# Rows spread to alternating channels, and zero products between the first maxima, in a two-layer gated attention and expert kernel

## The chip, the cores and the metric

The kernel runs on one core of one Trainium2 chip. The metric is the device time of one execution in microseconds, the median of several runs. The engines are named as in the profile: PE is the matrix engine (PEld its weight loads), DVE the vector engine, ACT the scalar engine, POOL the general engine, and SP the engine whose queue issues every DMA transfer of this kernel. Layers are counted 0 and 1, batches 0 to 7.

## The reference

The computation is two layers on x (8 batches of 100 tokens, 128 channels), each a cross-attention to a context of 1444 keys and then a mixture of experts:

```python
x = x + tanh(g_xattn[0]) * attention0(layernorm(x), ctx, mask)
x = x + tanh(g_ffn[0])   * experts0(layernorm(x))     # 64 experts of 64 channels, 8 per token, one shared
x = x + tanh(g_xattn[1]) * attention1(layernorm(x), ctx, energy gate)
x = x + tanh(g_ffn[1])   * experts1(layernorm(x))     # 8 experts of 352 channels, 2 per token
```

Attention has 16 heads of 8 channels with a softmax over the keys. An expert computes `down(silu(gate(x)) * up(x))`; a token's result is the sum over its experts, weighted with its routing weights. Both layers' experts are computed for all tokens, with weight 0 where a token is not routed to an expert.

## The kernel before

Each engine runs its own program, written out by hand; the order of an engine's instructions is the order in the code, and semaphores tie the engines together. There is no scheduler. The whole program is attention(0), experts(0), attention(1), experts(1).

**Attention.** For every batch, PE first finds the row maxima of the scores, head by head. A quad of maxima (`max_quad`, L1349) is four products of 100 x 482 into the four banks of `pm`; DVE takes them in two halves (`quad_max`, L487) into `mx_part`. A batch has 12 quads. From batch 1 on, the quads lie between the score products of the batch ahead (in `slots`). Those of batch 0 come ahead of everything, in the loop at the end of PE's `attention`: all 12 in layer 0, with three projections of keys (`k_chunk`) between them, and the last 8 in layer 1, since the first 4 are done inside experts(0) (`early_max`, L1556). After them `max_rows` turns the maxima, and the twelve slots of each batch follow: scores (L1405) to one of the two `ps` banks, exponent on ACT, weighted values on PE (L1426).

**Experts.** Channels are cut into units of 128: in layer 0 a unit is two experts of 64 channels, with the shared expert as the 33rd; in layer 1 there are 22 units. Tokens are cut into halves a and b (400 tokens), so layer 0 has 66 passes and layer 1 has 44, and pass n is called unit n here. Each unit goes round the engines:

- SP brings its weights (`wts`, a ring of 7, L1760) and its rows of routing weights (`wb`, a ring of 5, L1771 in layer 0, L1775 in layer 1). `wb` holds, for each of the 128 channels, the 400 routing weights of the expert that this channel belongs to. It comes from the array `routing` in DRAM, where an expert has one row of 400. SP issues the rows of unit n+5 when unit n has been weighted, and the weights of unit n+7 when the last product of unit n is done.
- ACT and DVE split the weights in a high and a low part (L1128, L648), PE multiplies (six products, L1611), ACT applies silu (L1136), DVE multiplies gate and up (L659).
- POOL multiplies the result with `wb` (`weigh`, L951, L961), and two units later PE adds the down product to the sum (`down`, L1640).

The layer-0 transfer is written so that the source is two rows, each repeated 64 times, and the outermost dimension has 2 entries:

```python
sp.dma_start(to[:], scratch[0][base + 2 * u:base + 2 * u + 2, :].unsqueeze(1)
             .broadcast_to([2, 64, HALF]))
```

The layer-1 transfers repeat one row over 128 channels, or two rows over two ranges of channels (96 and 32, or 64 and 64).

Beside its units, experts(0) carries work for layer 1 and for half b: the last steps of attention(0), the routing of half b (L754 to L815 on DVE at units 11 to 19, then one transfer of its rows to DRAM and back at unit 22), two context transfers (`ctxT`) at unit 22, keys and values of layer 1's batches 0 and 1 (`early_k`, L1536; `early_v`, L1546; units 30 to 50), the stacking of keys (`kst`, 24 transfers at units 36 to 39 and 53 to 56) and of queries (`qsel`, 12 transfers at units 47 to 49), and layer 1's first maxima (units 49 to 63).

Of the kernel before, what the change touches and what calls it, by code (L numbers as in the profile page):

```python
# [36 lines left out]
B, S, D = 8, 100, 128  # L37
# [17 lines left out]
HALF = TOK // 2  # L55
HB = B // 2

E0, F0 = 64, 64
# [10 lines left out]
W_RING, SPLIT_RING, WB_RING, H_RING = 7, 3, 5, 3  # L69
# [65 lines left out]
def experts_of(u):  # L135

    lo = 128 * u
    e = lo // I1
    cut = min(I1 * (e + 1) - lo, 128)
    return [(0, cut, e), (cut, 128, e + 1)] if cut < 128 else [(0, 128, e)]  # L140
# [29 lines left out]
def flamingo(nc, a, out, scratch):  # L170
    with ExitStack() as ctx:
        def sb(name, shape, dt=F32):
            return ctx.enter_context(nc.sbuf_tensor(name, shape, dt))
# [23 lines left out]
        zero_b = sb("zero_b", [128, 512], BF16)  # L197
# [95 lines left out]
        ps = ctx.enter_context(nc.psum_tensor("ps", [128, 2, 512], F32))  # L293
# [930 lines left out]
        def _(pe):  # L1224
            n = [0]
# [82 lines left out]
            def queries1(part):  # L1308
# [3 lines left out]
                step(nc.tensor.matmul(y_bank[part][:, 0:HALF], wq[1][:], xnT[:, b0 * S:b1 * S], start=True, stop=True),  # L1312
                     f"q1{part}")

            def attention(l):
                s = A[l]

                def k_chunk(b, c):
                    lo, w = CHUNKS[c]
                    if c == 0:  # L1320
                        pe.wait_ge(s["ctx_in"][b % 2], landed(b, b % 2, 2, 16))

                        if b >= 3:
                            pe.wait_ge(s["tail_step"], (b - 3) * TAIL + OUT_TAKEN)
                        elif b == 2:
                            pe.wait_ge(s["mrow_ready"], 1)
                            if l == 1:
                                pe.wait_ge(dve_done, marks["moe_out0b"])
                    else:
                        pe.wait_ge(s["klo_ready"], b * 3 + c)  # L1330
                    nc.tensor.matmul(pc[:, 0:w], wk[l][:], ctxT[b % 2][:, lo:lo + w], start=True,  # L1331
                                     stop=True).then_inc(s["kproj_done"], 1)
# [16 lines left out]
                def max_quad(b, k):  # L1349
                    n, (kind, j, x) = b * QUADS + k, MAX_QUADS[l][k]  # L1350
                    if k == 0:
                        pe.wait_ge(s["qbd_ready"], b + 1)
                        pe.wait_ge(s["khi_ready"], b * 3 + 3)
                        if b == 0:

                            pe.wait_ge(s["vraw_ready"], 2)
                            pe.wait_ge(s["klo_ready"], 3)
                    if l == 1 and 2 * n == EARLY_PAIRS:

                        pe.wait_ge(s["max_taken"], EARLY_PAIRS)  # L1360
                        pe.wait_ge(M[0]["prod_done"], 2 * UNITS0)

                    for i, bank in enumerate((0, 2, 1, 3) if kind == MAX_PAIR and b > 0 else (0, 1, 2, 3)):
                        g, c = (x + bank // 2, bank % 2) if kind == MAX_PAIR else (bank, x)
                        lo, rows = MAX_STARTS[c], slice(32 * g, 32 * g + 32)
                        first = l == 1 and 2 * n == EARLY_PAIRS
                        if n >= 1 and i == 0 and not first:
                            pe.wait_ge(s["max_taken"], 2 * n - 1)
                        if n >= 1 and bank == 2 and not first:
                            pe.wait_ge(s["max_taken"], 2 * n)  # L1370
                        mm = nc.tensor.matmul(pm[0:S, bank, 0:MAX_W], qbd[b % 2][rows, j * S:(j + 1) * S],  # L1371
                                              khi[b % 2][rows, lo:lo + MAX_W], start=True, stop=True,
                                              tile_position=(32 * g, 0))
                        if bank % 2 == 1:
                            mm.then_inc(s["chunk_ready"], 1)
# [129 lines left out]

                for k in range(0 if l == 0 else EARLY_PAIRS // 2, QUADS):
                    max_quad(0, k)
                    if l == 0 and k in FIRST_K_AFTER:
                        k_chunk(1, FIRST_K_AFTER.index(k))
                max_rows(0)  # L1510
# [159 lines left out]
        def _(sp):  # L1670
# [82 lines left out]
            def experts(l):  # L1753
                m, units = M[l], UNITS[l]
# [8 lines left out]
                def spread(n):  # L1763

                    v, u = n // units, n % units
                    if n >= WB_RING:

                        sp.wait_ge(m["weighted"], n - (WB_RING - 1))
                    base, to = v * ROUTE_ROWS[l], wb[n % WB_RING]
                    if l == 0:  # L1770
                        sp.dma_start(to[:], scratch[0][base + 2 * u:base + 2 * u + 2, :].unsqueeze(1)  # L1771
                                     .broadcast_to([2, 64, HALF])).then_inc(m["wb_in"][n % WB_RING], 16)
                    else:
                        for lo, hi, e in experts_of(u):
                            sp.dma_start(to[lo:hi, :], scratch[1][base + e:base + e + 1, :].broadcast_to([hi - lo, HALF]))\  # L1775
                                .then_inc(m["wb_in"][n % WB_RING], 16)
# [133 lines left out]
```

## Time and profile before

| | us |
|---|---|
| median of 3 runs | 1177.86 (1174.97 to 1178.06) |
| the profiled execution | 1178.84 |
| its span, first to last instruction | 1177.0 |
| PE busy | 980.1 (83%) |
| DVE busy | 685.9 (58%) |
| ACT busy | 529.9 (45%) |
| POOL busy | 270.8 (23%) |
| mean granted clock of PE | 0.863 of full speed |

The span falls in four stretches: attention(0) until about 400 us, experts(0) from there to 742, attention(1) to 1083, experts(1) to the end. The page's strip of 40 slices (29.4 us each) shows PE at 90% or more in most of attention and experts(1), and at 50% to 80% in experts(0); the granted clock is full in the first kind, apart from the very start and two slices of attention(1), and goes up and down in experts(0). The span is 1.84 us shorter than the profiled execution's own time, which is 0.98 us over the median.

### The profile page before, as it was taken

The numbers are of one execution on the slowest core, as the hardware profiler recorded it, in microseconds if no ns is written. First come the engines' busy times: TensorE is split into PE (matmuls) and PEld (weight loads), VectorE is DVE, ScalarE is ACT, GpSimd is POOL, SyncE is SP. The second block draws the span as 40 slices with busy tenths as digits, with TensorE's granted clock in tenths as the row PEclk, the third lists the DMA queues.
The fourth block names the chain that finished last, engine by engine and source line by source line (L and its number), as shares of the span: only waits on it lengthen the run. The fifth ranks groups of instructions, "written<-read, shape, count | busy, mean of one in ns | idle before, by whom it ended". The sixth has DMA issues, their size and how long they took to land.

```text
span 1177.0 us, 24416 instructions
## 1 busy us (share of the span) xinstructions
PE 980.1 (83%) x9702; PEld 637.3 (54%) x9702; DVE 685.9 (58%) x1428; ACT 529.9 (45%) x1152; POOL 270.8 (23%) x272
## 2 busy tenths in 40 slices
PE   5798999999999856764856766698999999998898
PEld 2255666666666544542543433255666665565686
DVE  7868676776775434421342332767577878762744
ACT  4045556656656512111312111045577777676443
POOL 3402012112111022221232322101023321321454
PEclk9588999999999987666897765557699999999999
DMA  7803142243031022223243343102144133311676
GB/s 194 194 2 82 22 103 59 52 97 86 18 77 49 19 78 91 83 81 117 89 119 102 101 117 112 31 2 61 39 102 96 47 76 92 78 49 46 170 201 155
DMA packets 47709, 99.73 MB, mean 85 GB/s; under 512 B 7494, under 2 KB 38419, under 8 KB 47596
## 3 DMA queue, kind: packets, MB, share of 16 engines
q1 hardware_dynamic: 47596, 98.18, 32.1%
q8 instruction: 76, 1.25, 0.4%
q14 instruction: 37, 0.30, 0.1%
HBM read 58.17 MB, written 0.65 MB: 50 GB/s over the span
## 4 chain that ended last, share of the span: by engine, by line
PE 30%; DMA 7%; issue 4%; DVE 3%; ACT 3%; SPq 2%; POOL 2%; POOLq 0%; DVEq 0%; ACTq 0%
PE ps L1405 10%; PE po L1426 7%; DMA wb<-routing 6%; PE pm L1371 3%; ACT probs L1049 2%; DVE mx_part L498 2%; PE ps L1611 2%; DMA wts<-in_experts 2%; PE po L1640 1%; PE pm L1611 1%; PE pc L1331 1%; PE pc L1344 1%; SPq L1760 1%; PE pm L1640 1%; POOL oraw L961 1%
## 5 line engine op out<-in xcount | busy, mean ns | idle before, releaser
L1049 ACT ACTIVATE probs<-ps 121x400 f32<-121x400 f32 (+1 forms) x768 | 356.7, 503 | 218.3 <-PE ps L1409 124.8
L1405 PE MATMUL ps<-qst,kst 128*121 128x400 f32 (+3 forms) x768 | 322.7, 466 | 26.9 <-ACT probs L1049 26.1
L498 DVE TENSOR_REDUCE mx_part<-pm 100x2 f32<-100x964 f32 x184 | 204.6, 1158 | 79.0 <-PE pm L1371 78.9
L1405 PEld LDWEIGHTS ps<-qst,kst 128*121 128x121 f32 (+3 forms) x768 | 143.4, 191 | 146.2 <-ACT probs L1049 90.3
L1426 PE MATMUL po<-probs,vaug 121*32 121x100 f32 x6144 | 180.7, 261 | 1.5 <-ACT probs L1049 1.5
L501 DVE CUSTOM_DVE_ANT_0 junk<-pm,negq 100x964 bf16<-100x964 f32 x128 | 143.6, 1158 | 52.0 <-PE pm L1371 51.6
L1426 PEld LDWEIGHTS po<-probs,vaug 121*32 121x32 f32 x6144 | 136.3, 114 | 55.2 <-ACT probs L1049 32.4
L648 DVE TENSOR_TENSOR w_lo<-wts,w_hi 128x256 fp32r<-128x256 f32 x110 | 52.9, 481 | 193.8 <-ACT w_hi L1128 193.5
L1128 ACT CAST w_hi<-wts 128x256 fp32r<-128x256 f32 x110 | 44.2, 402 | 232.8 <-DMA wts<-in_experts 232.7
L1371 PE MATMUL pm<-khi,qbd 32*100 32x482 f32 x752 | 128.6, 494 | 18.8 <-DVE mx_part L501 9.2
L1611 PE MATMUL ps<-qsel,w_hi 128*128 128x400 f32 x220 | 120.2, 546 | 11.3 <-DVE w_lo L648 11.3
L1409 PE MATMUL ps<-negT,ident_b 121*121 121x276 bf16 (+1 forms) x384 | 111.9, 291 | 0.0
L1371 PEld LDWEIGHTS pm<-khi,qbd 32*100 32x100 f32 x752 | 46.4, 176 | 82.7 <-issue 33.5
L505 DVE CUSTOM_DVE_ANT_0 junk<-pm,negq 100x482 bf16<-100x482 f32 x128 | 76.7, 655 | 22.7 <-PE pm L1371 22.6
L1136 ACT ACTIVATE tmpf<-ps 128x400 f32<-128x400 f32 x110 | 55.2, 502 | 76.8 <-PE ps L1611 76.7
L1611 PE MATMUL pm<-qsel,w_hi 128*128 128x400 f32 x220 | 88.3, 401 | 0.0
L892 POOL TENSOR_TENSOR qst<-qsel,early 96x400 fp32r<-96x400 f32 x64 | 53.0, 855 | 136.5 <-PE po L1426 122.9
L908 POOL TENSOR_TENSOR vaug<-vraw,early 121x512 f32<-121x512 f32 x24 | 26.8, 1118 | 220.0 <-ACT vraw L1073 215.5
L1611 PEld LDWEIGHTS ps<-qsel,w_hi 128*128 128x128 f32 x220 | 50.4, 229 | 37.4 <-DVE w_lo L648 22.4
L659 DVE TENSOR_TENSOR qhi<-pm,tmpf 128x400 f32<-128x400 f32 x55 | 31.5, 572 | 53.3 <-ACT tmpf L1136 38.3
L908 POOL TENSOR_TENSOR vraw<-vraw,late 121x512 f32<-121x512 f32 x24 | 26.3, 1097 | 143.4 <-ACT vraw L1073 143.4
L1409 PEld LDWEIGHTS ps<-negT,ident_b 121*121 121x121 bf16 (+1 forms) x384 | 53.2, 139 | 3.3 <-issue 3.3
(241 smaller groups left out, 1104.4 us busy)
## 6 DMA issues: line engine op xcount, KB each, us to landing
kst<-khi SPq DMA_DIRECT2D x128, 180.5 KB, 4.0
wts<-in_experts SPq DMA_DIRECT2D x110, 192.0 KB, 8.7
wb<-routing SPq DMA_DIRECT2D x98, 200.0 KB, 4.1
ctxT<-in_ctxT SPq DMA_DIRECT2D x16, 722.0 KB, 4.6
kst<-klo SPq DMA_DIRECT2D x64, 180.5 KB, 3.9
kst<-kst SPq DMA_DIRECT2D x7, 180.5 KB, 3.8
wb<-routing SPq DMA_DIRECT2D x8, 150.0 KB, 3.6
qsel<-qhi SPq DMA_DIRECT2D x8, 100.0 KB, 2.3
```

What stands on the lines that cost most here:

```text
L498: ins = nc.vector.tensor_reduce(parts[:, 2 * i:2 * i + 2, j, x], bank, AX, ALU.max)
L501: ins = nc.vector.tensor_tensor_reduce(junk[:, i], bank, mask, 1.0, -3e38, ALU.add, ALU.max, parts[:, x + i, j, 0:1])
L505: ins = nc.vector.tensor_tensor_reduce(junk[:, i, g % 2, :], pm[0:S, g, 0:MAX_W], negq[:, NK - MAX_W:NK], 1.0, -3e38, ALU.add, ALU.max, pa ...
L892: nc.gpsimd.tensor_tensor(qst[b % 2][0:96, g * GQ:(g + 1) * GQ].rearrange("p (j q) -> p j q", q=S), qsel[0:96, g, b * S:(b + 1) * S].unsqu ...
L908: nc.gpsimd.tensor_tensor(raw4 if l else dst, raw4, bias, ALU.add).then_inc(s["v_written"], 1)
L1049: nc.scalar.activation(probs[t % 2][0:r, g * GQ:(g + 1) * GQ], ps[0:r, n % 2, 0:GQ], ACT.Exp, scale=SCALE).then_inc(s["probs_ready"], 1)
L1136: nc.scalar.activation(sg[n % 2], gate_bank[n % 2][:, 0:HALF], ACT.Silu).then_inc(m["silu_done"], 1)
L1371: mm = nc.tensor.matmul(pm[0:S, bank, 0:MAX_W], qbd[b % 2][rows, j * S:(j + 1) * S], khi[b % 2][rows, lo:lo + MAX_W], start=True, stop=Tru ...
L1405: mm = nc.tensor.matmul(ps[0:r, n % 2, 0:GQ], kst[b % 2][0:rows, g, t * KEY_TILE:t * KEY_TILE + r], qst[b % 2][0:rows, g * GQ:(g + 1) * GQ ...
L1409: mm = nc.tensor.matmul(ps[0:r, n % 2, 0:GQ].rearrange("p (j q) -> p j q", q=S)[:, :, MASK_ROWS:S], ident_b[0:r, 0:r], negT[0:r, t, MASK_R ...
L1426: mm = nc.tensor.matmul(po[32 * j:32 * j + 32, g * S:(g + 1) * S], vaug[b % 2][0:r, t, 9 * h:9 * h + 32], probs[t % 2][0:r, h * S:(h + 1) ...
L1611: mm = nc.tensor.matmul(dst, w, x, start=(k == 0), stop=(k == 2))
```

## The change

Three edits. On PE, `occupy(3)` issues three products of zeros (128 x 128 by 400, bf16) into bank 1 of `ps`, which nobody reads then, after every quad of batch 0 but the first of layer 0: 11 times in layer 0, 8 times in layer 1. The layer-0 transfer of rows gets 64 entries in its outermost dimension, each of them the two rows one behind the other, so that row 0 goes to the even channels and row 1 to the odd ones. And the host lays the weights of layer 0 out in the same way, the channels of a unit's two experts alternating (the shared expert stays as it was, its two rows are both ones). Bytes, number of transfers and their places in SP's queue are the same.

```diff
+            def occupy(count):
+                for _ in range(count):
+                    nc.tensor.matmul(ps[:, 1, 0:HALF], zero_b[:, 0:128], zero_b[:, 0:HALF], start=True, stop=True)
...
                 for k in range(0 if l == 0 else EARLY_PAIRS // 2, QUADS):
                     max_quad(0, k)
+                    if k >= 1:
+                        occupy(3)
                     if l == 0 and k in FIRST_K_AFTER:
                         k_chunk(1, FIRST_K_AFTER.index(k))
...
                     if l == 0:
-                        sp.dma_start(to[:], scratch[0][base + 2 * u:base + 2 * u + 2, :].unsqueeze(1)
-                                     .broadcast_to([2, 64, HALF])).then_inc(m["wb_in"][n % WB_RING], 16)
+                        sp.dma_start(to[:], scratch[0][base + 2 * u:base + 2 * u + 2, :].unsqueeze(0)
+                                     .broadcast_to([64, 2, HALF])).then_inc(m["wb_in"][n % WB_RING], 16)
...
-    ex[:-1, :, 0] = i["L0_ffn_w1"].reshape(-1, 128, D).transpose(0, 2, 1)
-    ex[:-1, :, 1] = i["L0_ffn_w3"].reshape(-1, 128, D).transpose(0, 2, 1)
-    ex[:-1, :, 2] = i["L0_ffn_w2"].transpose(0, 2, 1).reshape(-1, 128, D)
+    woven = lambda w: w.reshape(-1, 2, F0, D).transpose(0, 2, 1, 3).reshape(-1, 128, D)
+    ex[:-1, :, 0] = woven(i["L0_ffn_w1"]).transpose(0, 2, 1)
+    ex[:-1, :, 1] = woven(i["L0_ffn_w3"]).transpose(0, 2, 1)
+    ex[:-1, :, 2] = woven(i["L0_ffn_w2"].transpose(0, 2, 1))
```

Where the zeros stand on PE in layer 0: the quads of batch 0 (products to `pm`) with the projections of keys (products to `pc`) between them. Before:

```order
L1258 MATMUL po<-early,ctxT 121x128 x4
L1371 MATMUL pm<-khi,qbd 100x482 x8
L1331 MATMUL pc<-ctxT,early 128x482
L1371 MATMUL pm<-khi,qbd 100x482 x8
L1331 MATMUL pc<-ctxT,early 128x482
```

And now, to the same projection (`ps<-zero_b` are the zeros; six more quads with zeros follow):

```order
L1258 MATMUL po<-early,ctxT 121x128 x4
L1376 MATMUL pm<-khi,qbd 100x482 x8
L1318 MATMUL ps<-zero_b 128x400 x3
L1336 MATMUL pc<-ctxT,early 128x482
L1376 MATMUL pm<-khi,qbd 100x482 x4
L1318 MATMUL ps<-zero_b 128x400 x3
L1376 MATMUL pm<-khi,qbd 100x482 x4
L1318 MATMUL ps<-zero_b 128x400 x3
L1336 MATMUL pc<-ctxT,early 128x482
```

Nothing changes places; each quad but the first has three products behind it that wait for nothing. On PE in layer 1, between the last product of experts(0) and the turning of the first maxima, before:

```order
L1640 MATMUL po<-oraw,wts 128x400
L1632 MATMUL po<-zero_b 128x400
L1371 MATMUL pm<-khi,qbd 100x482 x32
L1388 MATMUL pc<-early,rowmax 128x100
L1371 MATMUL pm<-khi,qbd 100x482 x8
```

and now (the first four of eight quads, the others likewise):

```order
L1647 MATMUL po<-oraw,wts 128x400
L1639 MATMUL po<-zero_b 128x400
L1376 MATMUL pm<-khi,qbd 100x482 x4
L1318 MATMUL ps<-zero_b 128x400 x3
L1376 MATMUL pm<-khi,qbd 100x482 x4
L1318 MATMUL ps<-zero_b 128x400 x3
L1376 MATMUL pm<-khi,qbd 100x482 x4
L1318 MATMUL ps<-zero_b 128x400 x3
```

Here too only the zeros are new. The two quads of batch 1 behind `max_rows` have none.

## Rows read from the trace of the kernel before

**Rows 1.** Tile `wb`, 395:742: its readers' engine sat idle until (us, times).
```profile
  DMA wb<-routing: 286.0, 65
```
**Rows 2.** Timeline of SP and POOL in experts(0): start, us, what [idle before <-releaser].
```profile
400.74 12.73 SPq L1771 DMA_DIRECT2D wb<-routing  x5
...
408.56 1.02 POOL L961 TENSOR_TENSOR tmpf<-qhi,wb 128x400 f32<-128x400 f32 x1 [46.84 <-DMA wb<-routing]
412.84 1.02 POOL L961 TENSOR_TENSOR hw<-qlo,wb 128x400 f32<-128x400 f32 x1 [3.26 <-DMA wb<-routing]
...
738.56 1.02 POOL L961 TENSOR_TENSOR oraw<-qlo,wb 128x400 f32<-128x400 f32 x1 [3.13 <-DMA wb<-routing]
```
**Rows 3.** Windows: us, busy PE, PEld, DVE, ACT, POOL; PEclk, DMA share, GB/s.
```profile
407.00:413.00 6.00, 2.70 (x13) 1.71 (x11) 1.20 (x3) 1.34 (x4) 1.18 (x2) 1.00 0.13 49
...
397.00:742.00 345.00, 221.96 (x747) 145.73 (x745) 106.81 (x264) 68.85 (x159) 88.37 (x88) 0.74 0.31 95
...
1133.00:1170.00 37.00, 36.58 (x166) 29.53 (x164) 18.97 (x40) 16.70 (x40) 22.30 (x22) 1.00 0.82 214
```
**Rows 4.** Timeline of POOL in experts(1), its first, two inner and last weighing.
```profile
1083.48 1.08 POOL L961 TENSOR_TENSOR tmpf<-qhi,wb 128x400 f32<-128x400 f32 x1 [37.99 <-DVE qhi L659]
...
1148.40 1.10 POOL L961 TENSOR_TENSOR hw<-qlo,wb 128x400 f32<-128x400 f32 x1 [0.67 <-PE po L1640]
1150.18 1.12 POOL L961 TENSOR_TENSOR oraw<-qhi,wb 128x400 f32<-128x400 f32 x1 [0.67 <-PE po L1640]
...
1169.68 1.02 POOL L961 TENSOR_TENSOR hw<-qlo,wb 128x400 f32<-128x400 f32 x1 [0.63 <-issue]
```
**Rows 5.** DMA: issues, KB each, median us to landing; last, all packets of 397:742.
```profile
wb<-routing SPq DMA_DIRECT2D x98, 200.0 KB, 4.1
ctxT<-in_ctxT SPq DMA_DIRECT2D x16, 722.0 KB, 4.6
...
DMA packets 19409, 32.75 MB, mean 95 GB/s; under 512 B 1732, under 2 KB 18244, under 8 KB 19396
```
**Rows 6.** Groups by form on PE, 397:742: busy us, mean ns | idle before.
```profile
L1550 PE MATMUL pc<-late,ctxT 128*121 128x128 f32 x48 | 8.2, 327 | 1.5 <-DVE klo L672 1.5
L1543 PE MATMUL pc<-ctxT,late 128*128 128x482 f32 x8 | 6.1, 858 | 8.3 <-DVE klo L672 7.8 <-issue 0.5
L1565 PE MATMUL pm<-khi,qbd 32*100 32x482 f32 x16 | 5.0, 625 | 0.0
...
L1543 PE MATMUL pc<-ctxT,late 128*128 128x480 f32 x4 | 2.3, 668 | 0.7 <-DVE klo L672 0.3 <-ACT vraw L1151 0.3
```
**Rows 7.** Waits in 397:742: us in total, times, longest.
```profile
PE pc L1543 <- DVE klo L672: 8.1, 3, 4.9
```
**Rows 8.** Windows: units 11 to 19 of experts(0), the routing of half b.
```profile
452.50:495.00 42.50, 28.57 (x98) 20.46 (x99) 21.22 (x84) 7.88 (x20) 9.25 (x9) 0.68 0.26 85
```
**Rows 9.** Groups by form, layer 1's first quads, 741:760, columns as above.
```profile
L498 DVE TENSOR_REDUCE mx_part<-pm 100x2 f32<-100x964 f32 x16 | 17.2, 1153 | 10.8 <-PE pm L1371 10.8
L1371 PE MATMUL pm<-khi,qbd 32*100 32x482 f32 x32 | 10.8, 718 | 5.8 <-DVE mx_part L498 5.8
...
L1632 PE MATMUL po<-zero_b 128*128 128x400 bf16 x1 | 0.5, 541 | 0.0
```
**Rows 10.** Windows: those quads, batch 0 of attention(1), batch 2 of it.
```profile
742.00:760.00 18.00, 10.57 (x33) 3.50 (x29) 17.40 (x17) 0.20 (x1) 1.69 (x3) 0.50 0.00 0
764.00:790.00 26.00, 24.96 (x211) 14.52 (x209) 17.08 (x34) 10.97 (x23) 0.00 (x0) 0.50 0.04 17
862.00:899.00 37.00, 35.55 (x522) 22.84 (x518) 29.68 (x32) 26.32 (x57) 10.50 (x11) 1.00 0.35 82
```
**Rows 11.** Timeline of PE: scores where batches 1, 2, 3 of attention(1) begin.
```profile
812.47 1.01 PE L1405 MATMUL ps<-qst,kst 97*113 97x400 f32 x2
...
862.09 0.77 PE L1405 MATMUL ps<-qst,kst 97*113 97x400 f32 x2
...
899.28 0.77 PE L1405 MATMUL ps<-qst,kst 97*113 97x400 f32 x2
```

## The prediction

> **What bounds the kernel now.** I read the table by windows first, because the share of busy time of the whole span hides that the four stretches have different limits. In experts(0) PE's granted clock is 0.74 on average and PE is busy 222 of 345 us, while the end of experts(1) has PE busy 36.58 of 37 us at full clock [rows 3]. So experts(0) is not held by PE. The view of one tile says by what: over the 66 units the engine that reads `wb` sat idle 286.0 us, 65 times, until a `wb` transfer had landed [rows 1]. POOL's timeline shows the pace: the first two units are weighed 4.28 us apart and each start is released by the DMA; from the first weighing (408.56) to the end of the last (738.56 + 1.02) it is 331.0 us, 5.0 us a unit [rows 2]. In experts(1) the same round (six products, silu, two products on DVE and POOL, a down product, 192 KB of weights and 200 KB of rows) takes 1.78 us a unit and POOL is released by PE [rows 4].
>
> Why `wb` is slow only in layer 0 is read from the DMA share. Between 407 and 413 us almost nothing but the first five `wb` transfers is under way; the 16 engines are then busy to 0.13, that is 2 of 16, moving 49 GB/s [rows 3]. 200 KB (204,800 bytes) at 49 GB/s is 4.2 us, which is the pace of POOL's starts [rows 2]. In experts(1), where a transfer of the same size has 128 (or 96 and 32) entries outermost, the share is 0.82 and 214 GB/s flow [rows 3]. So the two entries of the outermost dimension in layer 0 put each transfer on two engines, and the weights that share these two queue behind it.
>
> **Part 1, the transfer of rows.** With 64 entries outermost I take it that the transfer uses all 16 engines, as the layer-1 transfers do. No row shows 64 entries. The Trainium skill ("DMA: Bandwidth & Descriptors", section "Why a DMA increments its semaphore by 16 and not by 1") states that the number of engines is the largest one up to 16 that divides the outermost dimensions of source and destination: 2 for 2 entries on 128 channels, 16 for 64; for the 2 this trace agrees (0.13 of 16). Alternating the rows changes neither the 128 pieces nor their size, so I cost it at nothing; what covers it is experts(1), where one row is read 128 times at 214 GB/s.
>
> What is late next is PE, and the time of the stretch is built from experts(1):
> - Layer 1's 44 units took from 1083.48 to 1169.68 + 1.02, 87.2 us [rows 4]; this contains the last steps of attention, half b's norm and a smaller routing, and the return of its rows through DRAM.
> - 22 more units at 1.78: 39.2 us [rows 4].
> - Products that only experts(0) has (keys, values, first maxima of layer 1): 8.2 + 6.1 + 5.0 + 2.3 = 21.6 us busy at a mean clock of 0.74, so 16.0 at full clock [rows 3, 6].
> - These keys and values form a chain through one bank (PE, ACT, DVE, PE) at units 30 to 37. Before, three of its links made PE wait 8.1 us [rows 7]; now seven links follow at the pace of the units. Ends: 0, and 7 x 2.7 = 19 us. I take 9, since POOL's slower pace no longer covers them but the clock is higher.
> - DVE has 21.22 us of work in units 11 to 19 [rows 8]. A unit needs 18.97 / 37 x 1.78 = 0.91 of its time on DVE [rows 3], so nine units need 8.2 and the routing 13.0; nine units leave 9 x 0.87 = 7.8 idle. 5.2 us stick out. Ends: 0 and 13.
> - Two contexts of 722 KB stand in SP's queue directly behind the rows of unit 27: a landing takes 4.6 us [rows 5], two 9.2, against a lead of `wb` that the return of half b's rows has just used up. I take 5; ends 0 and 9.
> - Rank products, transposes and queries, and the SP queue with 24 key and 12 query transfers: 6; ends 0 and 21. The bytes set a floor for it all: 32.75 MB [rows 5] at 214 GB/s is 153 us.
>
> Sum: 87.2 + 39.2 + 16.0 + 9 + 5.2 + 5 + 6 = 167.6, call it **168 us**, above the 153 of the bytes. Ends: 142 (no waits, DMA over 214 GB/s) and 204 (the upper ends). The first weighing also comes earlier: the five transfers were issued from 400.74 and the first had landed at 408.56, 7.8 us later [rows 2]; the median landing of 200 KB is 4.1 [rows 5], so 3.7 us. Gain: 331.0 + 3.7 - 168 = **166.7 us**; ends 193 and 131.
>
> **Part 2, the zeros.** One product of zeros alone took 0.54 us at half clock [rows 9], so three cost at most 1.6. In layer 1's first quads DVE is the bound: 16 halves of 1153 ns in 17.2 us, one every 1.07, and PE waits 5.8 us for DVE in between [rows 9]. Zeros behind a quad lie in that wait as long as they and the quad's own two halves (0.72 each) fit in 2.14 us; 1.44 + 0.70. The 0.54 contains the fill of an isolated product; three in a row need less each, so little or nothing sticks out; at worst 8 x 0.9 = 7 us. In layer 0 the same, with three projections of keys in PE's way as well: between 5 us lost and 5 won, taken as 1 won.
>
> What they can bring is clock. Those quads ran at 0.50, and so did batch 0 for its next 26 us, although PE was busy 24.96 of them; batch 2 ran at 1.00 [rows 10]. Batch 1, with a half-clock stretch in it, took 49.6 us and batch 2 37.2 [rows 11]; batch 0 (764 to 812.5) was 11 over as well. So at most 11 + 12.4, call it 24 us, is there. Experts(0), PE-bound, should now hand over a full clock where it handed over half. But PE was busy 10.57 of 18 us in the quads, and the clock did not rise in the 26 dense microseconds behind them [rows 10]; a full clock that falls there once is paid for long. Batch 1's loss starts from waits inside batch 0 that the zeros do not touch. I take 5 of 24, nearer to the row that shows no rise; ends 0 and 24.
>
> A rule that speaks against a gain is in the Trainium skill ("TensorE: Matmul & The Clock Gate", section "A second HAM failure mode: psum-queue depth-cycling"): short pauses of PE between groups that cycle through PSUM banks make the clock go to and fro. By that rule the 5 would be 0 and the time 1010; the trace has such a pattern in experts(0), whose clock is 0.74, and none with zeros between.
>
> **The rivals.**
> - *The clock holds through the quads into batches 0 and 1.* Then 24 instead of 5 is won: 986. For it: PE is now the bound ahead of the quads. Against it: the 26 us at half clock with PE busy.
> - *The freed units run at half clock.* For it: 0.74 in experts(0) [rows 3]. A unit then takes 2 x 1.78 and the stretch 66 x 3.56 + 41 = 276; gain 331.0 + 3.7 - 276 = 59, time 1113. Against it: experts(1) with the same products is at 1.00.
> - *The transfer stays on two engines.* Then only the zeros act: 1178.84 - 6 is 1173, 1172 against the median. For it: no row with 64 entries. Against it: the layer-1 rows.
> - *Slower: the transfer stays on two engines and the zeros stand in the way of the maxima.* At 0.54 each, three need 1.62 where 0.70 is free: 0.9 a quad, 19 quads, 17 us: 1178.84 + 17 is 1196. It decides from 0.23 us a product upwards, at half clock, and only where nothing else is won.
>
> **How the numbers follow.** 1178.84 - 166.7 - 5 - 1 = 1006.1 for a profiled execution, and the median lies 0.98 under it: **1005 us**. Ends of the sum: 1005 - 26 - 19 - 4 = 956 and 1005 + 36 + 5 + 6 = 1052. Chances: the forecast with its ends 0.75, the clock that holds 0.19, half clock 0.03, no engines won 0.02, slower 0.01. The range 973 to 1042 leaves out the outermost part of both ends and the last three cases, about 2 in 10. All but the last two cases are faster by over 0.3% (what a measurement here can tell from no change), and a gain of 6 us is too: faster 0.98, same 0.01, slower 0.01.
>
> **What would show it.** In the changed profile: `wb` waits of POOL in experts(0) under 60 us instead of 286; POOL there released by PE, DVE or PE's bank; a DMA share of 0.5 or more; a stretch of about 168 us with its longest stops at units 12 to 18, 27 to 29 and 30 to 37. Granted clock near 1 in experts(0). In the first quads of layer 1, DVE still starting every 1.07 us with the zeros in PE's gaps; batch 0 of attention(1) either near 40 us (clock held) or near 48. I am wrong if the DMA share in the first microseconds of `wb` is again 0.13, if the units run at 3.5 us, or if the context and key transfers, not PE, set the stretch, which then would be 190 us or more.

## The result, and the profile after

| | before | after |
|---|---|---|
| median, us | 1176.41 (4 runs, 1169.05 to 1178.06) | 1012.6 (4 runs, 1004.36 to 1042.33) |
| ratio after / before | | 0.8595, 95% interval 0.8522 to 0.8667 |
| profiled execution, us | 1178.84 | 1004.36 |
| its span, us | 1177.0 | 1002.5 |
| mean granted clock of PE | 0.863 | 0.944 |

The run of 1042.33 had a lower mean granted clock than the other three (0.898 against 0.931 to 0.944), and the ratio leaves it out. The forecast was 1005, with 973 to 1042 as its range.

Where the 174.5 us between the two profiled executions went, by the times at which each part begins and ends in the two traces:

| stretch | before, us | after, us | difference |
|---|---|---|---|
| start to the first scores of attention(0) | 61.77 | 65.61 | +3.8 |
| first scores to the first weighing of experts(0) | 346.79 | 343.14 | -3.65 |
| first weighing to the end of the last, experts(0) | 331.03 | 169.07 | -162.0 |
| from there to the first weighing of experts(1) | 343.89 | 333.17 | -10.7 |
| experts(1) | 87.23 | 85.13 | -2.1 |

The page of after, its engine line and two strips of 40 slices (25.1 us each):

```profile
PE 911.5 (91%) x9759; PEld 600.6 (60%) x9759; DVE 688.1 (69%) x1428; ACT 529.4 (53%) x1152; POOL 276.0 (28%) x272
...
PEclk9559799999999999999999967889999999999999
DMA  6830505142250410456577900044144144105675
```

The stretch of low digits that experts(0) had in the clock strip is gone. What is left below 9 are slices 2, 3 and 5, at the start, and slices 24 to 27, which are layer 1's first quads and the batches behind them. The view of tile `wb` in after, 395:580, answers [rows 1] (us, times):

```profile
  DMA wb<-routing: 65.1, 13
  DVE qlo L659: 18.7, 10
  PE pm L1647: 13.8, 11
```

286.0 us in 65 waits have become 65.1 in 13, and 43.4 of these are the one wait ahead of the first weighing, in which attention(0) was still at work. So inside the stretch the transfer holds POOL for 22 us of 169; in the kernel before, with the 46.84 ahead of its first weighing left out in the same way, it was 239 of 331. The timeline of SP and POOL in after answers [rows 2]; the columns are start, us, engine, line, operation and the idle time before it with its releaser:

```profile
405.51 3.21 SPq L1778 DMA_DIRECT2D wb<-routing  x5
...
408.75 1.08 POOL L961 TENSOR_TENSOR tmpf<-qhi,wb 128x400 f32<-128x400 f32 x1 [43.35 <-DMA wb<-routing]
410.06 1.09 POOL L961 TENSOR_TENSOR hw<-qlo,wb 128x400 f32<-128x400 f32 x1 [0.23 <-DVE qlo L659]
...
459.58 1.10 POOL L961 TENSOR_TENSOR tmpf<-qlo,wb 128x400 f32<-128x400 f32 x1 [0.65 <-PE pm L1647]
461.35 1.11 POOL L961 TENSOR_TENSOR hw<-qhi,wb 128x400 f32<-128x400 f32 x1 [0.66 <-PE pm L1647]
...
487.05 1.09 POOL L961 TENSOR_TENSOR oraw<-qhi,wb 128x400 f32<-128x400 f32 x1 [2.77 <-PE pm L1647]
490.91 1.09 POOL L961 TENSOR_TENSOR tmpf<-qlo,wb 128x400 f32<-128x400 f32 x1 [2.77 <-PE pm L1647]
...
576.79 1.03 POOL L961 TENSOR_TENSOR oraw<-qlo,wb 128x400 f32<-128x400 f32 x1
```

The first weighing comes 3.24 us after SP begins to issue, where it was 7.8. Units 21 and 22 stand 1.77 us apart and PE releases POOL, which is the pace and the releaser of experts(1) in [rows 4]. Units 32 and 33 (487.05 and 490.91) stand 3.86 us apart: there PE makes keys and values of layer 1 between the units. Windows of after (busy PE, PEld, DVE, ACT, POOL; granted clock, DMA share, GB/s) answer [rows 3, 10]:

```profile
400.00:578.00 178.00, 151.43 (x761) 112.81 (x750) 108.62 (x264) 68.34 (x159) 90.60 (x85) 0.98 0.65 184
...
582.10:612.80 30.70, 27.70 (x130) 11.52 (x132) 24.70 (x24) 6.24 (x12) 0.86 (x1) 0.50 0.08 25
612.80:643.60 30.80, 26.45 (x360) 15.24 (x352) 26.30 (x49) 18.39 (x40) 0.00 (x0) 1.00 0.00 1
643.60:660.60 17.00, 16.36 (x158) 9.93 (x158) 10.12 (x12) 7.19 (x16) 4.11 (x5) 0.50 0.57 129
```

In experts(0) the DMA share rose from 0.31 to 0.65, the clock from 0.74 to 0.98. In layer 1's quads and in attention(1) two stretches are still at half clock, 30.7 and 17.0 us long. The weights gained too: the page's median from issue to landing of a `wts` transfer is 3.2 us in after and was 8.7.

### The profile page after: what moved, and what is told of

Same layout as the page of the kernel before. It is cut to its first block and busy times, and to the rows that moved or that the text cites. A ratio compares the mean times of both kernels' runs of the same rounds, so it can differ in the third digit from the quotient of the medians.

```text
span 1002.5 us, 24530 instructions
## 1 busy us (share of the span) xinstructions
PE 911.5 (91%) x9759; PEld 600.6 (60%) x9759; DVE 688.1 (69%) x1428; ACT 529.4 (53%) x1152; POOL 276.0 (28%) x272
## 5 line engine op out<-in xcount | busy, mean ns | idle before, releaser
L1410 PE MATMUL ps<-qst,kst 128*121 128x400 f32 (+3 forms) x768 | 315.6, 456 | 28.0 <-ACT probs L1049 26.9
L1410 PEld LDWEIGHTS ps<-qst,kst 128*121 128x121 f32 (+3 forms) x768 | 140.1, 187 | 142.9 <-ACT probs L1049 88.5
L1431 PE MATMUL po<-probs,vaug 121*32 121x100 f32 x6144 | 176.7, 257 | 1.5 <-ACT probs L1049 1.5
L1431 PEld LDWEIGHTS po<-probs,vaug 121*32 121x32 f32 x6144 | 133.3, 112 | 54.4 <-ACT probs L1049 32.0
L1376 PE MATMUL pm<-khi,qbd 32*100 32x482 f32 x752 | 124.5, 481 | 10.4 <-DVE mx_part L501 5.8
L1618 PE MATMUL ps<-qsel,w_hi 128*128 128x400 f32 x220 | 101.4, 461 | 20.7 <-DVE w_lo L648 20.6
L1618 PE MATMUL pm<-qsel,w_hi 128*128 128x400 f32 x220 | 76.6, 348 | 0.0
L659 DVE TENSOR_TENSOR qhi<-pm,tmpf 128x400 f32<-128x400 f32 x55 | 31.5, 572 | 53.8 <-ACT tmpf L1136 43.4
L1618 PEld LDWEIGHTS ps<-qsel,w_hi 128*128 128x128 f32 x220 | 42.0, 191 | 42.6 <-DVE w_lo L648 31.3
L659 DVE TENSOR_TENSOR qlo<-pm,tmpf 128x400 f32<-128x400 f32 x55 | 31.6, 574 | 35.1 <-ACT tmpf L1136 27.2
```

Source lines behind the costliest of these rows:

```text
L659: nc.vector.tensor_tensor(tu[n % 2], up_bank[n % 2][:, 0:HALF], sg[n % 2], ALU.mult).then_inc(m["prod_done"], 1)
L1410: mm = nc.tensor.matmul(ps[0:r, n % 2, 0:GQ], kst[b % 2][0:rows, g, t * KEY_TILE:t * KEY_TILE + r], qst[b % 2][0:rows, g * GQ:(g + 1) * GQ ...
L1431: mm = nc.tensor.matmul(po[32 * j:32 * j + 32, g * S:(g + 1) * S], vaug[b % 2][0:r, t, 9 * h:9 * h + 32], probs[t % 2][0:r, h * S:(h + 1) ...
L1618: mm = nc.tensor.matmul(dst, w, x, start=(k == 0), stop=(k == 2))
```

## The experiments

Each is an edit of the kernel after, or of it without the zeros; zeros_only is an edit of the kernel before. The last four columns are read from the one profiled execution of each kernel. "Start" is the time of the first scores of attention(0), "experts(0)" the time from its first weighing to the end of its last; batches 0 and 1 are those of attention(1). The runs were on several chips, on which the kernel before had medians of 1172.7 to 1176.6 us (one run of 1172.89 beside six_layer1 and ones_layer1), so kernels are better compared by the ratio than by the time.

| kernel | median, us | ratio to before, 95% | start | experts(0) | batch 0 | batch 1 |
|---|---|---|---|---|---|---|
| before | 1176.4 | | 61.8 | 331.0 | 49.0 | 49.5 |
| after | 1012.6 | 0.8595 (0.8522 to 0.8667) | 65.6 | 169.1 | 44.9 | 42.1 |
| both_again | 1013.69 | 0.8629 (0.8595 to 0.8662) | 64.6 | 170.8 | 45.1 | 47.7 |
| rows_only | 1008.95 | 0.8597 (0.8552 to 0.8641) | 60.5 | 168.9 | 45.0 | 47.6 |
| zeros_layer1 | 1009.07 | 0.8589 (0.8556 to 0.8622) | 61.3 | 171.8 | 45.0 | 47.6 |
| zeros_only | 1180.17 | 1.0041 (1.0016 to 1.0067) | 63.3 | 329.8 | 50.2 | 47.9 |
| four_entries | 1046.38, one run | | 61.9 | 211.3 | 44.8 | 42.1 |
| eight_entries | 1024.88, one run | | 61.8 | 183.5 | 45.1 | 47.7 |
| two_transfers | 1020.5 | 0.8676 (0.864 to 0.8711) | 61.6 | 181.8 | 49.1 | 47.7 |
| spaced | 998.52 | 0.8492 (0.8458 to 0.8525) | 62.4 | 156.4 | 45.0 | 47.6 |
| six_layer1 | 1004.29, one run | | 60.4 | 168.9 | 45.1 | 47.8 |
| ones_layer1 | 1004.58, one run | | 60.5 | 167.4 | 45.0 | 47.6 |
| no_stop | 993.26 | 0.8439 (0.8395 to 0.8484) | 62.0 | 159.6 | 42.3 | 37.9 |
| no_stop_zeros | 991.61 | 0.842 (0.8378 to 0.8462) | 60.9 | 158.8 | 42.2 | 47.0 |

### The parts of the change apart

**both_again** is the kernel after once more, beside the next three.

> The changed kernel once more, as the yardstick of this chip: 1004 to 1015 us by either theory, experts(0) from the first weighing to the end of the last 169 us (168 to 171), first scores of attention(0) at 65.6 us, batches 0 and 1 of attention(1) 37 to 49 us each, as the clock falls in that execution.

**rows_only** has no `occupy` at all:

```diff
                     max_quad(0, k)
-                    if k >= 1:
-                        occupy(3)
```

> The transfer with 64 entries and no zeros at all. Theory T (the transfer alone brings the gain, and the zeros only stand in PE's way in layer 0): experts(0) again 169 us, first scores of attention(0) back at 61.8 us as before, 3.8 us earlier than with zeros; attention(1) within 5 us of the changed kernel; 1000 to 1010 us, about 4 under the yardstick. Theory Z (the zeros brought the 11 us that attention(1) lost): attention(1) goes back to the 344 us it took before, the whole is 1008 to 1018, 5 to 8 over the yardstick.

**zeros_layer1** keeps the zeros in layer 1 alone (`if l == 1: occupy(3)`).

> The transfer with 64 entries, zeros in layer 1's quads only. Theory T: first scores of attention(0) at 61.8 us, layer 1's quads 2.4 us each where the clock is half and 2.1 where it is full, so 0 to 2 us slower than without zeros; 1001 to 1011 us. Theory Z: this is the best of the four, 1000 to 1008 us, with attention(1) 10 us shorter than without zeros.

**zeros_only** keeps both sets of zeros, with the transfer and the weights of before.

> The zeros in both layers, with the old transfer of 2 entries and the old layout of weights. Theory T: 3.8 us lost in layer 0, experts(0) 331 us as before, layer 1's quads at half clock and 2 us longer: 1178 to 1184 us, not faster than before. Theory Z: attention(1) wins about 11 us, less 3.8: 1167 to 1172 us.

The transfer alone brings the whole gain: 0.8597 without any zeros, 0.8629 with both sets. The zeros alone make the kernel before slower by 0.41%, 4.8 us, and that interval excludes 1. One place where they cost is the start: without zeros in layer 0 the first scores came at 60.4 to 62.4 us in eleven traces, with them at 63.3, 64.6 and 65.6 (61.4 and 64.5 in the mean). The other is layer 1's quads: in zeros_only the first scores of attention(1) came 26.0 us after the end of experts(0), and 24.4 in before. Two windows, of before and then of after, from the first quad to the first scores:

```profile
20.80:61.80 41.00, 27.86 (x64) 9.77 (x64) 34.58 (x76) 10.14 (x11) 18.80 (x15) 0.56 0.80 184
```

```profile
20.80:65.60 44.80, 37.55 (x97) 12.95 (x96) 34.71 (x76) 10.14 (x11) 18.99 (x16) 0.56 0.75 169
```

DVE's work is the same (34.6 and 34.7 us), and so is the clock (0.56). PE is busy 9.7 us longer. PE's timeline in after shows why the zeros found no room:

```profile
30.36 1.18 PE L1318 MATMUL ps<-zero_b 128*128 128x400 bf16 x3
31.78 2.28 PE L1376 MATMUL pm<-khi,qbd 32*100 32x482 f32 x4 [0.23 <-DVE mx_part L505]
33.99 1.18 PE L1318 MATMUL ps<-zero_b 128*128 128x400 bf16 x3
34.96 1.81 PE L1336 MATMUL pc<-ctxT,early 128*128 128x482 f32 x2
36.71 1.13 PE L1376 MATMUL pm<-khi,qbd 32*100 32x482 f32 x4
```

From 31.78 to 37.77 PE does not stop: three zeros (1.18 us, 0.39 each, at half clock), a projection of 1.8 and two quads. Before, PE was idle for 13.1 of the 41.0 us, and 3.2 of these lay behind the first quad, where there are no zeros. Eleven times 1.18 us (13.0) don't fit in the other 9.9, and DVE waits in its turn.

### Whether it is the number of engines, and whether the alternation is needed

Both kernels are rows_only with another shape of the transfer and the weights in the old order. **four_entries**:

```diff
-    sp.dma_start(to[:], scratch[0][base + 2 * u:base + 2 * u + 2, :].unsqueeze(0)
-                 .broadcast_to([64, 2, HALF]))
+    sp.dma_start(to[:], scratch[0][base + min(2 * u, 62):base + min(2 * u, 62) + 4, :].unsqueeze(1)
+                 .broadcast_to([4, 32, HALF]))
```

> No zeros, the old order of channels, and a transfer with 4 entries outermost: four neighbouring rows, each repeated 32 times, so that the weights are not the right ones; bytes and pieces are the same. Theory E (the outermost entries set the number of engines): DMA share of about 0.25 and 98 GB/s while only the rows are under way, the first rows 2.1 us apart, and units of 2.7 us (32 pieces of rows at 67 ns and 8 of weights on each of four engines), experts(0) 195 to 215 us, the whole 1035 to 1055 us. Theory A (it is the alternation or the layout that made it fast, not the engines): 331 us as before, 1176 us.

**eight_entries** is the same with eight rows and `[8, 16, HALF]`.

> As with 4 entries, but 8 rows, each repeated 16 times (again not the right weights). Theory E: share about 0.5 and 196 GB/s while only the rows are under way; 16 pieces of rows and 8 of weights are 1.6 us for an engine, under PE's 1.77, so experts(0) is 169 to 180 us, the whole 1005 to 1022 us. Theory A: 331 us, 1176 us.

With two entries a unit took 4.72 us, with four 2.67, with eight 1.76, and with 64 also 1.76 (each over units 20 to 26). POOL's timeline in four_entries says what holds it:

```profile
472.41 1.04 POOL L961 TENSOR_TENSOR tmpf<-qhi,wb 128x400 f32<-128x400 f32 x1 [1.50 <-DMA wb<-routing]
475.00 1.04 POOL L961 TENSOR_TENSOR hw<-qlo,wb 128x400 f32<-128x400 f32 x1 [1.55 <-DMA wb<-routing]
477.65 1.05 POOL L961 TENSOR_TENSOR oraw<-qhi,wb 128x400 f32<-128x400 f32 x1 [1.61 <-DMA wb<-routing]
```

Each start is again released by the DMA. With twice the entries a unit takes 0.57 of the time, and the pace goes by the number of entries until PE takes over at 1.76. The DMA share while little but the first rows is under way goes by it too; windows of four_entries, of eight_entries and of after (columns as above):

```profile
408.00:411.00 3.00, 2.74 (x15) 2.00 (x14) 1.65 (x5) 0.80 (x2) 1.49 (x2) 1.00 0.26 100
408.00:411.00 3.00, 1.96 (x12) 1.46 (x11) 2.35 (x7) 1.58 (x6) 1.07 (x1) 1.00 0.43 153
408.00:410.00 2.00, 0.96 (x6) 0.63 (x5) 1.93 (x6) 0.99 (x4) 1.08 (x1) 1.00 0.94 280
```

Of 16 engines 0.26 are 4.2, 0.43 are 6.9 and 0.94 are 15.0; with two entries it was 0.13 [rows 3], which are 2.1. Eight entries reach PE's pace in the plain units, but the stretch as a whole (183.5) was over the 169 to 180 expected, and the time (1024.88) over the 1005 to 1022: beside rows_only it lost 3.3 us in units 26 to 30, 7.4 in units 40 to 49 and 3.5 in the last 17. At these places POOL waits for `wb` in both kernels, and longer with eight entries (9.5 against 6.1 us at units 27 to 30, 8.3 against 2.1 at 43 to 47, 18.7 against 15.7 at 55 to 62). So the rows are late there again; why was not tried.

**two_transfers** leaves the channels as they were and sends each of the two rows with a transfer of its own, 64 entries each (the count of landings to wait for is doubled with it):

```diff
...
+    for i in range(2):
+        sp.dma_start(to[64 * i:64 * i + 64, :], scratch[0][base + 2 * u + i:base + 2 * u + i + 1, :]
+                     .broadcast_to([64, HALF]))
```

> No zeros, the old order of channels, and two transfers for each unit, of one row repeated 64 times each. Theory E: all 16 engines again, experts(0) 168 to 175 us in spite of one more issue of 0.5 us on SP for each unit; 1003 to 1015 us, the same as with one transfer of 64 entries. Theory A: no alternation, so 4 us a unit or more and over 1100 us.

It gets the plain units to 1.76 too, so the alternation is a means and not the cause. But its stretch is 181.8, a miss by 7 to 14 us, and its kernel is slower than rows_only (0.8676 against 0.8597, with intervals that just touch). SP's timeline in it, where keys are stacked:

```profile
512.65 0.59 SPq L1793 DMA_DIRECT2D kst<-khi  x1
513.28 0.59 SPq L1793 DMA_DIRECT2D kst<-klo  x1
513.92 0.60 SPq L1793 DMA_DIRECT2D kst<-khi  x1
514.56 0.62 SPq L1765 DMA_DIRECT2D wts<-in_experts  x1
515.22 1.64 SPq L1777 DMA_DIRECT2D wb<-routing  x2
516.90 0.59 SPq L1793 DMA_DIRECT2D kst<-khi  x1
```

The queue has no gap: a round of three stacks, a weight and two rows takes SP 4.25 us (512.65 to 516.90), so here the issuing of transfers sets the pace of the units. One transfer for both rows saves one of these six issues. The alternation of channels, which makes one transfer possible, is worth 12.9 us of the stretch (181.8 against 168.9, one trace each): 4.0 in units 26 to 30, 1.8 in units 30 to 40, 2.4 in units 40 to 49 and 4.7 in the last 17. That the issuing costs all of it is not shown.

### The stretch's longest term

**spaced** is rows_only with the keys and values of layer 1 at other units; the two contexts come at units 24 and 29 and the stacks at every second unit:

```diff
-EARLY_K = [UNITS0 - 3, UNITS0 - 2, UNITS0 - 1, UNITS0 + 1, UNITS0 + 2, UNITS0 + 4]
-EARLY_V = [UNITS0, UNITS0 + 3, UNITS0 + 6, UNITS0 + 9, UNITS0 + 13, UNITS0 + 17]
+EARLY_K = [30, 32, 34, 38, 40, 42]
+EARLY_V = [36, 44, 46, 48, 50, 52]
...
-EARLY_QBD, EARLY_QST, EARLY_QSEL, EARLY_KST = [UNITS0 + 14, UNITS0 + 18], UNITS0 + 20, UNITS0 + 14, [UNITS0 + 3, UNITS0 + 20]
+EARLY_QBD, EARLY_QST, EARLY_QSEL, EARLY_KST = [UNITS0 + 14, UNITS0 + 18], UNITS0 + 20, UNITS0 + 14, [36, 50]
...
```

> The transfer with 64 entries, no zeros, and the work for layer 1 inside experts(0) set further apart: the two contexts behind units 24 and 29 instead of both behind 22, keys and values at least two units apart (30, 32, 34, 38, 40, 42 and 36, 44, 46, 48, 50, 52), a stack of keys every second unit. If the terms of the sum are right (the chain of keys and values 9 us, the contexts 5, part of the stacks 6), experts(0) falls from 169 to 155 (150 to 160) and the whole to 995 (989 to 1001). If the bytes set the stretch instead, it stays at 165 or more and the whole at 1005.

The waits of 478:516 in rows_only (us in total, times, longest) have links of the chain, and POOL's timeline there the pace:

```profile
PEld pc L1548 <- DVE klo L672: 5.5, 3, 2.0
```

```profile
484.66 1.09 POOL L961 TENSOR_TENSOR tmpf<-qlo,wb 128x400 f32<-128x400 f32 x1 [2.77 <-PE pm L1645]
488.59 1.09 POOL L961 TENSOR_TENSOR hw<-qhi,wb 128x400 f32<-128x400 f32 x1 [2.84 <-PE pm L1645]
```

And POOL's in spaced, a unit with no key and then one with a key ahead of it:

```profile
481.63 1.10 POOL L961 TENSOR_TENSOR tmpf<-qlo,wb 128x400 f32<-128x400 f32 x1 [1.43 <-PE pm L1645]
483.41 1.09 POOL L961 TENSOR_TENSOR hw<-qhi,wb 128x400 f32<-128x400 f32 x1 [0.67 <-PE pm L1645]
486.14 1.11 POOL L961 TENSOR_TENSOR oraw<-qlo,wb 128x400 f32<-128x400 f32 x1 [1.64 <-issue]
```

In rows_only the units from 30 to 40 take 2.9 to 4.2 us; in spaced, up to unit 38, those with a key or a value take 2.3 to 3.1 and the others 1.4 to 2.0. Units 30 to 40 fall from 36.0 to 25.3 us, and the units behind them, which take over some of the links, do not rise (62.8 and 61.3). So these 10.7 us of the stretch were not work but links standing behind each other. 6.8 of them lie in units 30 to 35, ahead of the first stack, where the links share one bank; in the other 3.9 the run does not part the links from the stacks, which moved too. The contexts' move gained nothing: units 26 to 30 took 10.2 us in it and 10.5 in rows_only, and POOL's waits for `wb` there were 5.9 and 6.1. At 0.8492 (0.8458 to 0.8525) spaced beats rows_only and the kernel after (both_again).

### The clock in layer 1's quads

rows_only and zeros_layer1 differ only in the 24 zeros there, and both have two stretches of 30.7 us at half clock, the first from the quads into batch 0 (576.2 to 606.9 and 581.1 to 611.8). So three zeros a quad do not hold it. Two kernels ask whether three were too few or zeros the wrong data; both are rows_only with `if l == 1: occupy(...)` behind a quad. **six_layer1** has six zeros, **ones_layer1** three products of ones.

> The transfer with 64 entries, and behind each of layer 1's eight quads six products of zeros instead of three (none in layer 0). With three, PE's clock fell 3 us after the quads began and stayed at half for 30.7 us, as it did without any. Theory G (too little work: more of it holds the clock): the clock stays full through the quads, each 2.1 us, batch 0 of attention(1) takes 37 to 41 us instead of 45, the whole 1000 to 1006 us. Theory N (zeros do not hold it, whatever their number): the clock falls as before; a quad at half clock then has 6 x 0.33 + 1.4 = 3.4 us of PE, eight take 27 us instead of 19, and the whole is 1012 to 1020 us.

> The same with three products of ones by ones (none of zeros, none in layer 0). Theory V (products of zeros do not count as work, products of other values do): the clock stays full through layer 1's quads, batch 0 of attention(1) takes 37 to 41 us, the whole 1000 to 1006 us. Theory G: three of either kind are too little: the clock falls within 7 us of the quads' start and stays at half for 30.7 us, batch 0 takes 45, the whole 1006 to 1012 us, as with three products of zeros.

Windows of the quads and the start of batch 0, of rows_only and then of six_layer1 (columns as above):

```profile
576.00:593.20 17.20, 10.57 (x33) 3.54 (x31) 15.92 (x17) 0.79 (x2) 0.96 (x2) 0.51 0.00 0
593.20:596.00 2.80, 1.31 (x4) 0.48 (x4) 2.80 (x3) 0.74 (x1) 0.00 (x0) 0.50 0.51 138
596.00:606.80 10.80, 10.28 (x88) 6.22 (x86) 7.09 (x10) 4.71 (x10) 0.00 (x0) 0.50 0.09 35
```

```profile
576.00:593.20 17.20, 14.12 (x73) 5.93 (x73) 16.30 (x17) 1.14 (x2) 0.86 (x1) 1.00 0.00 1
593.20:596.00 2.80, 1.93 (x6) 0.96 (x6) 2.80 (x4) 0.38 (x1) 0.00 (x0) 0.50 0.60 194
596.00:606.80 10.80, 10.28 (x87) 6.01 (x85) 6.87 (x10) 4.71 (x10) 0.00 (x0) 0.50 0.05 20
```

Six zeros kept the clock at 1.00 through the quads, in the trace of one execution. It bought nothing. In these two kernels DVE sets the pace of the quads at either clock (busy 16.30 and 15.92 of 17.2 us), and at 593.2, between the last quad and the first scores, the clock fell all the same; batch 0 had its 10.8 us at half clock as before (45.1 us against 45.0). Three ones left the clock at 0.51 in the same window, so at that number, in one trace each, the values made no difference.

At half clock three are not free either. From the end of experts(0) to the first scores of attention(1) it is 23.2 us in rows_only, 22.9 with six zeros at full clock, and 24.8 with three products in after, both_again, zeros_layer1 and ones_layer1. PE's timeline in after:

```profile
586.91 1.18 PE L1318 MATMUL ps<-zero_b 128*128 128x400 bf16 x3
588.02 1.36 PE L1376 MATMUL pm<-khi,qbd 32*100 32x482 f32 x4
589.31 1.18 PE L1318 MATMUL ps<-zero_b 128*128 128x400 bf16 x3
```

A quad with its zeros takes 2.40 us here, where DVE alone needs 2.14 (two halves of 1.07, [rows 9]): PE has become the bound.

### The half clock in batch 1

The second stretch of 30.7 us falls on batch 1 (47.6 us where batch 3 takes 37.2), and no zeros touch it. About 3 us ahead of it PE stops once for 1.5 us, since two operations for half b's queries stand ahead of the row maxima on DVE. The wait is in batch 0 of all twelve traces that have these operations in this order, and in each of them the clock falls 1.5 to 2.5 us after PE goes on; PE's waits in spaced, 585.2:630:

```profile
PE pc L1393 <- DVE rowmax L515: 1.5, 1, 1.5
```

**no_stop** is spaced without this stop: the queries come one slot earlier, and two of their three operations on DVE stand behind the row maxima.

```diff
-LAST_OUT_SLOT, LAST_TURN_SLOT, LAST_QUERIES_SLOT = 1, 8, 9
+LAST_OUT_SLOT, LAST_TURN_SLOT, LAST_QUERIES_SLOT = 1, 7, 8
...
                             row_max(b + 1)
+                            if l == 1 and b == 0:
+                                queries1_split("b")
```

> The spaced version (998.5 us) with one thing moved: inside batch 0 of attention(1) the queries of half b come one slot earlier, and two of their three operations on DVE stand behind the row maxima instead of ahead of them. In the spaced version PE stops there 1.5 us for DVE's row maxima, about 3 us before the clock falls to half for 30.7 us, which falls on batch 1 (47.6 us where batch 3 takes 37.2). Theory S (this stop is what the half clock follows): the stop is under 0.5 us, no half clock there, batch 1 at 37 to 39 us and the time 987 to 990. Rival D (a fall comes there anyway, whatever PE does in that slot): batch 1 again 47.6, time 997 to 999.

**no_stop_zeros** adds zeros: six behind each of layer 1's first quads, ten behind the last, six and two behind the two quads of batch 1 that follow.

> The version with the moved queries, and zeros again in layer 1's first maxima: six behind each quad, ten behind the last, six and two behind the two quads of batch 1 that follow. With six a quad the granted clock stayed at 1.00 through the quads and fell to 0.50 only 3 us ahead of the first scores, so that batch 0 still had its 11 us at half. If zeros in the two stops between the quads and the scores carry the clock on, batch 0 goes from 45.0 to 39 to 41 us, and the time is 4 to 6 us under the version without zeros. If the clock falls at the first scores all the same, it is within 1.5 us of that version.

The stop is gone in both; PE's timeline in no_stop shows the transposition of the row maxima (L1399) with no idle time marked:

```profile
625.97 0.44 PE L1416 MATMUL ps<-qst,kst 97*121 97x400 f32 x1
626.45 0.31 PE L1399 MATMUL pc<-early,rowmax 100*128 100x100 f32 x1
```

The windows behind it, of no_stop and then of no_stop_zeros:

```profile
599.20:629.00 29.80, 26.81 (x365) 15.55 (x369) 26.26 (x46) 19.11 (x41) 0.00 (x0) 1.00 0.01 3
629.00:660.00 31.00, 29.58 (x417) 18.38 (x405) 26.12 (x30) 20.98 (x45) 6.24 (x7) 1.00 0.42 93
```

```profile
597.20:631.30 34.10, 30.63 (x418) 17.66 (x417) 30.75 (x50) 22.02 (x47) 1.14 (x2) 1.00 0.04 11
631.30:655.20 23.90, 23.58 (x207) 14.39 (x205) 12.30 (x15) 9.79 (x20) 2.96 (x4) 0.50 0.49 107
```

In the profiled execution of no_stop the clock holds and batch 1 takes 37.9 us, as theory S had it. In that of no_stop_zeros it falls, with no such stop ahead of it, 7.2 us after the same product, and batch 1 takes 47.0. The stop is therefore not needed for the fall. The other executions spread in the same way: of six of no_stop two took 981.4 and 984.0 us at mean clocks of 0.949 and 0.951, and four took 991 to 1000 at 0.928 to 0.936; no_stop_zeros had two of 982 at 0.960 and 0.963 and four of 991 to 997 at 0.940 to 0.951. All six of spaced are at 0.925 to 0.936 (993 to 1003). So in four executions of twelve without the stop, and in none of six with it, the time was about 10 us lower. That and the fall right behind the stop in twelve traces point to the stop as one thing that favours the fall; so few runs don't prove it, and spaced ran on a chip on which the kernel before was 4 us slower. What else decides it is open. The median of no_stop, 993.26, missed the 987 to 990 of theory S and the 997 to 999 of its rival; the intervals of its ratio and that of spaced overlap.

The zeros between the quads and batch 0 failed: the clock was 1.00 through the quads and fell at the first scores, and batch 0 took 42.2 us with them and 42.3 without. The drop of batch 0 from 45.0 to 42.3 comes from the moved queries.

## Why the prediction was right, and where it was wrong

**The bound and its cause: right.** `wb` in experts(0) was on two engines, and more entries take it off. The pace by two, four and eight entries (4.72, 2.67, 1.76), the DMA share under the first rows (0.13, 0.26, 0.43, and 0.94 with 64) and two_transfers, which has no alternation and the same 1.76, show it. By the Trainium skill's rule ("DMA: Bandwidth & Descriptors", section "Why a DMA increments its semaphore by 16 and not by 1") four entries use four engines, eight use eight and 64 all of them. The traces agree with shares of 0.26 and 0.94; the 0.43 of eight entries is under the 0.5 of eight engines at work without a pause.

**The length of the stretch: right in its sum, 168 against 169.07; the terms are looser.** The pace of 1.78 was 1.76. Units 11 to 20, with half b's routing, took 24.5 us where nine at 1.76 are 15.8: 8.7 over, against a term of 5.2. The first 11 units were another 5.2 over, and the 87.2 us taken over from layer 1 held 8.9 more than 44 units at 1.78; so over the first 20 units the sum met the size (14.1 and 13.9). Units 26 to 30 took 11.5 against 7.0, 4.5 over, where the contexts had 5; but spaced moved the contexts and gained nothing there, so the size was met while the reason is in doubt. The chain of keys and values was put at 9, between 0 and 19, and spaced won 11 there. No run measures the remaining 6 for ranks and stacks by itself. In the last 17 units, 8.9 us over, POOL waits for `wb` again, 12.9 us in eight waits at units 55 to 62; the longest:

```profile
562.06 1.05 POOL L961 TENSOR_TENSOR oraw<-qlo,wb 128x400 f32<-128x400 f32 x1 [2.98 <-DMA wb<-routing]
```

There SP issues the second set of stacks and has no gap in its queue, as in two_transfers. So the next bound at the stacks is SP's issuing, which the prediction named only by its number of transfers.

**The start of experts(0): right, in part by luck.** 3.7 us were forecast; the stretch ahead of it shrank by 3.65. The 4.1 us of landing that it stood on are a median over 98 transfers, 66 of which are the slow ones of layer 0. From SP's first issue to the first weighing it became 3.24 us, 4.6 less, but SP began to issue 0.9 us later after the first scores.

**The zeros in layer 0: wrong in sign.** The prediction took 1 us won, between 5 lost and 5 won; it is 3.8 lost in this trace, 3.1 between the means of the traces with and without zeros there, and 4.8 by the ratio of zeros_only over both layers. The step that failed is "in layer 0 the same": the working for layer 1, where DVE has 2.14 us a quad, was carried over to a place where PE had projections of 1.8 to 2.0 us between the quads and little idle time.

**The zeros in layer 1: near, on the cost side.** At most 7 us were allowed; 1.6 were lost (24.8 against 23.2), because at half clock a quad with its three zeros (1.18 us, where 0.70 was free) takes 2.40 us on PE and 2.14 on DVE; six of the eight quads in after were longer, by 0.26 each.

**The clock: 5 us forecast, 10.7 seen, and not from the zeros.** In the kernel without any zeros that stretch between the experts shrank by 7.0 us (343.89 to 336.91), and with zeros by 4.9 in both_again and 5.4 in zeros_layer1. The gain is there without the zeros: batch 0 is 4 us and batch 1 2 us shorter in rows_only, and the quads 1.2. How long batch 0 takes goes with how much of it is at half clock: 26.1 us of 49.0 in before, where the half clock began 31 us ahead of the end of experts(0), and 10.8 of 45.0 in rows_only, where it began 3 us behind it. That a full clock handed over by experts(0) brings this is argued, not shown, and it is not enough: in two_transfers the clock was full at the end of experts(0), yet the half clock behind it lasted 44.4 us, and batch 0 took 49.1. The rest of the 10.7 is one execution: after's second stretch at half clock lasted 17.0 us and not 30.7, and batch 1 took 42.1 us; both_again, with the same instructions, had 30.7 and 47.7. This luck of the profiled execution is likely also why it lies at 1004 and the median at 1013 (its mean clock was 0.944, and 0.937 and 0.931 in the runs of 1010 and 1015). The rival in which the clock holds through the quads did not come; the case in which the zeros win nothing came nearest.

**Of what was to show it:** the `wb` waits were to be under 60 us and were 65.1, because the 43.4 ahead of the first weighing count among them (22 inside the stretch); POOL was released by PE and DVE, and at units 27, 28, 44, 45 and 55 to 62 also by the transfer; the longest stops lay at units 11 to 20, 26 to 30 and 30 to 40 and, not foreseen, in the last 17 units (38.8 us, where 17 at 1.76 are 29.9). DVE starting every 1.07 us in the quads was wrong: it started after 1.08 and 1.33 us in turn. Batch 0 was to take about 40 us or about 48 and took 44.9, with 10.2 us of it at half clock.

## What to carry to other kernels

When one transfer paces a stretch, look at the DMA share while little else is under way: it tells how many engines the transfer uses, and the outermost dimension of the access pattern can be made longer without more transfers, if the data is laid out to suit it. Then the issuing queue's time per transfer and chains through one bank are what is late next; count them at their busiest units, not over the stretch. Filler work for the clock has to be shown to raise the clock and to lie in idle time at the clock that is really granted there; here it did the first only at twice the number, and then where PE was not the bound.

## What was not expected of the hardware

The same instructions ran at either clock in different executions. In the profiles the half-clock stretch that falls on batch 1 lasted 30.7 or 30.8 us in nine (both_again, rows_only, zeros_layer1, zeros_only, eight_entries, two_transfers, spaced, six_layer1, ones_layer1), 34.1 in before, 17.0 in after and in four_entries, 23.9 in no_stop_zeros, and was absent in no_stop. Whole or absent it makes 10 us, 1% of the time, which is more than most of the terms in dispute here.
